# Selective scan beside a mixture of experts: decaying states kept in PSUM, every read-out on VectorE, one product for ranks and rows

## What is computed

```python
# L3 attention (E = 256 channels, N = 16 states, rank 64, after an RMS norm and a causal convolution)
xs    = silu(conv(x @ in_w.T) + conv_b)
delta = softplus(xs @ wd1.T @ wd2.T + wd2_b)
A     = -exp(A_log)                      # 256 x 16
Bm, Cm = xs @ wb.T, xs @ wc.T            # 16 numbers per token each
# per token l, channel e, state n:
h[e,n] = exp(delta[e] * A[e,n]) * h[e,n] + (delta[e] * xs[e]) * Bm[n]
y[e]   = sum over n of h[e,n] * Cm[n]
out    = resid + ((y + xs * W_D) * silu(skip)) @ out_w.T
# L3 ffn: 8 experts, 128 -> 512 -> 128, relu, top-p gates; every expert runs on every token
y = sum over e of gate[e] * (relu(x @ W1[e] + b1[e]) @ W2[e] + b2[e])
```

## Time and profile before

| | us |
|---|---|
| median of 3 runs | 2452.4 |
| lowest, highest | 2448.72, 2458.42 |
| the profiled execution, its own time | 2451.05 |
| its span, first to last instruction | 2449.3 |
| TensorE busy (share of the span) | 2167.2 (88%) |
| VectorE busy | 1669.1 (68%) |
| ScalarE busy | 1234.2 (50%) |
| GpSimd busy | 1018.8 (42%) |
| first scan starts, last scan starts | 1560.2, 2327.2 |

### The profile page before, as it was taken

One profiled execution on the slowest core, in us unless ns is written; L12 is line 12 of the kernel. 1 busy time (PEld: TensorE's weight loads), 2 busy tenths in 40 slices (PEclk: granted clock), 3 DMA queues, 4 the chain that ended last, 5 costly groups with the idle time before them and its releaser, 6 DMA issues. The chain is left out here.

```text
span 2449.3 us, 33072 instructions
## 1 busy us (share of the span) xinstructions
PE 2167.2 (88%) x11302; PEld 1547.8 (63%) x11302; DVE 1669.1 (68%) x3253; ACT 1234.2 (50%) x2710; POOL 1018.8 (42%) x815
## 2 busy tenths in 40 slices
PE   7888777899799999999997595767999999999998
PEld 3565556688698988898897484322554545545554
DVE  6667555677666676667765694599687877869921
ACT  6231222499544454554453352556566565655543
POOL 5000000121122233233322463689687777868722
PEclk9799899899899999999998696898999999999999
DMA  9500000000000000000000234333333324334311
GB/s 352 165 1 0 1 1 1 1 1 1 20 1 1 1 11 11 1 11 11 9 4 11 68 104 161 97 112 97 108 104 96 113 91 117 110 94 121 95 35 35
DMA packets 77151, 145.25 MB, mean 59 GB/s; under 512 B 9432, under 2 KB 31080, under 8 KB 75944
## 3 DMA queue, kind: packets, MB, share of 16 engines
q1 hardware_dynamic: 72600, 133.67, 17.7%
q0 software_dynamic: 4384, 9.46, 1.2%
HBM read 130.91 MB, written 31.65 MB: 66 GB/s over the span
## 5 line engine op out<-in xcount | busy, mean ns | idle before, releaser
L224 ACT ACTIVATE TMP<-ps,W 128x512 f32<-128x512 f32 (+2 forms) x784 | 457.1, 614 | 391.5 <-PE ps L209 225.6
L209 PE MATMUL ps<-TMP,W 128*128 128x512 f32 (+5 forms) x1232 | 612.8, 604 | 42.3 <-ACT TMP L227 9.4
L209 PE MATMUL ps<-TMP 128*128 128x65 f32 (+5 forms) x4354 | 514.9, 286 | 6.6 <-DVE W L229 4.4
L209 PEld LDWEIGHTS ps<-TMP 128*128 128x128 f32 (+3 forms) x4354 | 474.6, 192 | 52.5 <-issue 17.5
L233 POOL TENSOR_TENSOR TMP<-TMP 128x512 f32<-128x512 f32 (+1 forms) x176 | 227.9, 1298 | 588.0 <-ACT TMP L224 435.6
L209 PEld LDWEIGHTS ps<-TMP,W 128*128 128x128 f32 (+3 forms) x1232 | 218.3, 188 | 250.7 <-issue 152.8
L233 POOL TENSOR_TENSOR TMP<-TMP,W 128x512 f32<-128x512 f32 x256 | 356.9, 1418 | 30.4 <-DVE TMP L2874 29.3
L209 PE MATMUL ps<-TMPr,Wr 128*128 128x512 f32 x768 | 320.0, 524 | 5.6 <-ACT TMP L224 5.6
L209 PE MATMUL ps<-TMPr 128*128 128x512 f32 (+4 forms) x1032 | 266.3, 404 | 34.0 <-DVE TMPr L229 23.1
L209 PEld LDWEIGHTS ps<-TMPr 128*128 128x128 f32 (+2 forms) x1032 | 192.9, 197 | 84.3 <-issue 23.2
L209 PEld LDWEIGHTS ps<-TMPr,Wr 128*128 128x128 f32 x768 | 145.0, 190 | 140.9 <-issue 116.0
(11 more groups left out here) (239 smaller groups left out, 3114.3 us busy)
## 6 DMA issues: line engine op xcount, KB each, us to landing
W<-rows SPq DMA_DIRECT2D x224, 256.0 KB, 3.6
sorted<-pad SPq DMA_DIRECT2D x8, 2304.0 KB
XK<-gates SPq DMA_DIRECT2D x64, 256.0 KB, 3.5
TMP<-rows SPq DMA_DIRECT2D x32, 256.0 KB, 3.3
TMP<-sorted SPq DMA_DIRECT2D x72, 72.0 KB, 2.0
W<-wp SPq DMA_DIRECT2D x1, 4124.0 KB, 14.8
XK<-results SPq DMA_DIRECT2D x16, 256.0 KB, 3.8
W<-wp SPq DMA_DIRECT2D x1, 3072.0 KB, 27.1
```

The costliest lines, as they stand in the source:

```text
L209: return nc.tensor.matmul(out, lhsT, rhs, start=start, stop=stop, **k)
L224: return nc.scalar.activation(out, x, f, bias=bias, scale=scale)
```

## The change

- The scan writes its result over its own decay operand, `Ab[x]` in PSUM; the four buffers `Hb` are gone.
- Every read runs on VectorE, right behind its scan in the list, with `Ab[x]` (PSUM) as its second operand; `by_pool` and GpSimd's reads are gone. There are 8 buffers `Cb` instead of 6.
- `carry` reads the last column from `Ab[x]` and waits for the read; `decay` of the next state waits for the read of the state before, and for the carry's copy, where there is one.
- `rank` and `bc` become one product with 96 output rows (`wnT`), copied by one `rank_out` into one of two tiles `Nw`. `delta` multiplies all 96 rows, with zeros in the 32 rows of `wd2T` that face B and C; `rows_out` stores rows 64 to 95.
- `first_unit` is 59 instead of 58, and most steps beside are one slot later.
- `tail` of a slot comes 4 slots after its scan (as before), `output` one slot later than before.

```diff
-     ... ("wd1T", 128, 128), ("wd2T", 64, 256), ("wd2b", 128, 2), ("wbcT", 128, 64), ...
+     ... ("wnT", 128, 192), ("wd2T", 96, 256), ("wd2b", 128, 2), ...
-        Bb, Cr, Ub, Hb, Cb = (more(n) for n in (4, 4, 6, 4, 6))
-        narrow = ar(512)
-        d1, Bw = narrow[0:64, :], [narrow[64 + 32 * j:96 + 32 * j, :] for j in range(2)]
+        Bb, Cr, Ub, Cb = (more(n) for n in (4, 4, 6, 8))
+        Nw = [ar(512) for _ in range(2)]
-        by_pool = lambda g: g % 16 % 3 == 1
-        first_unit = 32 + 26
+        first_unit = 32 + 27
-            put(q + 8, ("rank", i))
-            put(q + 9, ("rank_out", i), ("bc", i))
-            put(q + 10, ("bc_out", i))
+            put(q + 9, ("rank", i))
+            put(q + 10, ("rank_out", i))
...
             if 0 <= g < GN:
-                plan.append(("scan", (g, s)))
-                if s:
-                    plan.append(("read", (g, 0)))
+                plan += [("scan", (g, s)), ("read", (g, s))]
             plan += gated(u - 2) + joined(u - 3)
-            if 0 <= g - 2 < GN:
-                plan.append(("tail", (g - 2, s)))
-                if (g - 2) % 16 == 15:
-                    plan.append(("output", ((g - 2) // 16, s)))
+            if 0 <= q - 4 < 2 * GN:
+                plan.append(("tail", divmod(q - 4, 2)))
+            if 0 <= q - 5 < 2 * GN and (q - 5) // 2 % 16 == 15:
+                plan.append(("output", ((q - 5) // 32, (q - 5) % 2)))
             plan += beside.pop(q, [])
             if 0 <= g + 1 < GN:
                 plan.append(("decay", (g + 1, s)))
-            if s and 0 <= g < GN:
-                plan.append(("read", (g, 1)))
             plan += down(u - 1)
...
                     for x in range(2):
-                        r = mm(bank(step, a)[0:64, :], w("wd1T")[:, x * 64:(x + 1) * 64], ch(sets[a % 2][1], x), x == 0, x == 1)
+                        r = mm(bank(step, a)[0:96, :], w("wnT")[:, 96 * x:96 * x + 96], ch(sets[a % 2][1], x), x == 0, x == 1)
...
-                    mm(bank(step, a), tile(w("wd2T"), x), d1).then_inc(*de_pe(a))
+                    mm(bank(step, a), tile(w("wd2T"), x), Nw[i % 2][0:96, :]).then_inc(*de_pe(a))
...
-                e.wait_ge(*h_dve.at((g, x)))
-                acopy(car[:, j:j + 1], Hb[(2 * g + x) % 4][:, 511:512]).then_inc(*c_act((g, x)))
+                e.wait_ge(*hc_dve.at((g, x)))
+                acopy(car[:, j:j + 1], Ab[x][:, 511:512]).then_inc(*c_act((g, x)))
...
                     if g:
-                        e.wait_ge(*h_dve.at((g - 1, x)))
+                        e.wait_ge(*hc_dve.at((g - 1, x)))
+                        if (g - 1) // 16 % 2 == 0:
+                            e.wait_ge(*c_act.at((g - 1, x)))
                     act(Ab[x], ch(sets[i % 2][2], x), ACT.Exp, scale=negA[:, x * 16 + n:x * 16 + n + 1]).then_inc(*a_act(a))
...
-                    nc.vector.tensor_tensor_scan(Hb[q % 4], Ab[x], Ub[q % 6], first, ALU.mult, ALU.add).then_inc(*h_dve(a))
-                elif step == "read" and not by_pool(a[0]):
+                    nc.vector.tensor_tensor_scan(Ab[x], Ab[x], Ub[q % 6], first, ALU.mult, ALU.add).then_inc(*h_dve(a))
+                elif step == "read":
                     g, x = a
                     q = 2 * g + x
                     e.wait_ge(*h_dve.at(a))
...
-                    tt(Cb[q % 6], Cr[g % 4], Hb[q % 4], ALU.mult).then_inc(*hc_dve(a))
+                    tt(Cb[q % 8], Cr[g % 4], Ab[x], ALU.mult).then_inc(*hc_dve(a))
...
-                    gtt(Cb[q % 6], Cr[g % 4], Hb[q % 4], ALU.mult).then_inc(*hc_pool(a))
```

More of the change, by code:

```diff
@@ L2365, in hand_over @@
             n = norm(7, i)
[L2366 to L2384, removed]
+            put(q + 6, ("out", i))
+            put(q + 7, ("result", i))
+            put(q + 8, n[0])
+            put(q + 9, n[1])
+            put(q + 10, n[2])
+            put(q + 11, n[3])
+            put(q + 13, n[4])
+            put(q + 14, n[5])
+            put(q + 15, n[6])
+            put(q + 16, n[7], ("split", i))
+            put(q + 17, ("shift", i))
+            put(q + 19, ("probs", i))
+            put(q + 20, ("route", (i, 0)))
+            put(q + 21, ("route", (i, 1)))
+            put(q + 23, ("route", (i, 2)))
+            put(q + 25, ("row", i))
+            put(q + 26, ("row_out", i))
+            put(q + 28, ("table", i))
+            put(q + 29, *[("fetch", 8 * i + k) for k in range(3)])
         def norm_ahead(i, q):
@@ L2407, in scan_moe_stage @@
         plan += both("shut") + norm(6, 1)[:3]
-        plan += [("rank", 0), ("bc", 0), ("rank_out", 0), ("bc_out", 0)] + both("delta")
+        plan += [("rank", 0), ("rank_out", 0)] + both("delta")
         plan += [("softplus", (0, 0)), ("softplus", (0, 1)), ("exp", 0), ("log", 0), ("dx", 0), ("rows_out", 0)]
@@ L2483, in scan_moe_stage @@
         I = range(NCH)
-        rk_pe, rk_act, bc_pe, ex_act, ln_act, dl_dve, dx_pool, out_pe, res_dve = (
-            Sig(sem("s7_" + n), I) for n in ("rank_pe", "rank", "bc_pe", "delta_exp", "delta_log", "delta", "dx", "out_pe", "out"))
+        rk_pe, rk_act, ex_act, ln_act, dl_dve, dx_pool, out_pe, res_dve = (
+            Sig(sem("s7_" + n), I) for n in ("rank_pe", "rank", "delta_exp", "delta_log", "delta", "dx", "out_pe", "out"))
         de_pe, mx_act, ab_act = (Sig(sem("s7_delta_" + n), of(plan, "delta")) for n in ("pe", "max", "abs"))
@@ L2489, in scan_moe_stage @@
         GE = [(g, e) for g in G for e in range(2)]
[L2490 to L2493, removed]
+        a_act, u_pool, h_dve, hc_dve, y_pe = (Sig(sem("s7_" + n), GE) for n in ("decay", "input", "state", "read", "y_sum"))
         c_act = Sig(sem("s7_carried"), [(g, e) for g, e in GE if g // 16 % 2 == 0])
@@ L2520, in scan_moe_stage @@
         for s, a in plan:
-            if s in ("open", "conv", "rank", "bc", "delta", "centre", "back", "back2", "logits", "out", "row"):
+            if s in ("open", "conv", "rank", "delta", "centre", "back", "back2", "logits", "out", "row"):
                 takers.append((s, a))
-        first_bank = {("conv", (0, 0)): 7, ("conv", (0, 1)): 5, ("rank", 0): 6, ("bc", 0): 4, ("delta", (0, 0)): 7, ("delta", (0, 1)): 5,
+        first_bank = {("conv", (0, 0)): 7, ("conv", (0, 1)): 5, ("rank", 0): 6, ("delta", (0, 0)): 7, ("delta", (0, 1)): 5,
                       }
@@ L2532, in scan_moe_stage @@
             holder[bank_no(*t)] = t
-        let_go = {"open": gt_dve, "conv": ev_act, "rank": rk_act, "bc": raw_act, "delta": ab_act, "back": n_xa, "back2": n_xk,
+        let_go = {"open": gt_dve, "conv": ev_act, "rank": rk_act, "delta": ab_act, "back": n_xa, "back2": n_xk,
                   "logits": n_lgs, "out": res_dve, "row": rw_act}
```

81 lines of the change are left out of this document (29 added, 52 removed), and 2 rows, old and new, of the table GROUPS.

## The result

The changed kernel takes 2464.3 us (median of 7 runs, 2461.2 to 2465.8), the kernel before, beside it on the same chip, 2452.4: a ratio of 1.0042, with an interval of 1.0029 to 1.0055. The forecast was 2431, in a range of 2412 to 2460, and the measured time lies above that range. It became slower, by a little less than the 0.5% that I had taken for measurable, though the interval lies wholly above 1. The profiled execution took 2462.4 us around a span of 2460.6, against 2451.1 and 2449.3.

A forecast was written before the change was run, and what follows sets the result against it. VectorE and GpSimd were taken to bound the lead, VectorE the routing stretches, TensorE the rest. The terms -4.7 - 6.0 - 8.6 - 1.0 + 1.1 - 1 (last 32 scan slots) gave -20.2, so 2431 us, range 2412 to 2460.

The forecast's parts named there:

- One slot later: Whole last stage: a lead slot more (2.4), a common slot less (3.3), an end slot more (2.0); +1.1 us.
- Routing stretches: VectorE-bound stretch of each 32-slot block in the common part: reads -0.7, contention -1.0, chain +0.7; six stretches, -6.0 us.
- three hand-overs between engines: In the chain from scan over read and ScalarE to the next decay: about 0.08 us each, an estimate.
- The lead: First 56 scans, bound by VectorE and GpSimd: reads -4.7, decay waits +2, less contention -2; -4.7 us in all.
- a bound of 12: Sign of being wrong: VectorE waiting more than 12 us for decays in the lead, against 6.9 before.
- One product: One matmul product less per chunk, 1.7 us: -8.6 where TensorE bounds, -1.0 ahead of the first scan.
- The scan in PSUM: Every scan: writing its output to PSUM costs 0 more, taken from ScalarE's rows.
- That rival: Scan pays for its output in PSUM: 1.74 us per scan, 2494 us in all, slower; chance 0.12.
- The dependent pair: Each read right behind its scan: gap 0.03, no overlap; 0.12 us per slot, 6.7 in the lead.
- the rival without it: A dependent read costs no more than any other: lead 6.7 less, six routing stretches 1.0 each, 2418; chance 0.06.
- The rival by ScalarE's chain: Each of 24 long ScalarE stays costs the lost slack, 1.1 us; 2451, no change; chance 0.15.

The follow-up runs named there:

- e1: The changed kernel with all steps beside back in their old slots (first_unit 58); 2445.1 us, ratio 0.9977 to the kernel before.
- e4: The kernel before with `rank` and `bc` as one product with 96 rows and nothing else; 2435.6 us, ratio 0.9934 to the kernel before.
- e8b: e1 with each slot's read moved behind the steps beside, as the slot's last VectorE work; ratio 0.9932 to the kernel before.
- e7: The changed kernel with only `open`, its copy and its gate one slot later; 2446.3 us, ratio 0.9952 to the kernel before.
- e5b: e5a with each read right behind its scan, states still in SBUF; ratio 1.0075 to the kernel before.
- e5c: e5b with decay and carry waiting for the read in place of the scan, states in SBUF; ratio 1.008 to the kernel before.
- e5a: e4 with all reads on VectorE at their old places in the list, states in SBUF; 2449.9 us, ratio 0.9976 to the kernel before.
- e13: The changed kernel with only each slot's decay moved ahead of its steps beside in the lists; ratio 0.9982 to the kernel before.

## Why the prediction was wrong

**One slot later, +1.1: the step that failed, by 18 us.** I priced the slots by their mean lengths. e1 measures the move at 19.6 us in the changed kernel (16 by the ratios). What a slot holds was to be read, not how long it is: the change moves `log` one slot and leaves `square` and `open`, so ScalarE's 3.7 us between the table loads now end in what TensorE needs next. The rule that I had written down myself, what stands behind a long stay in an engine's list and who waits for it, I applied to the decay and not to the moved steps.

**Routing stretches, -6.0: wrong in sign.** From e4 to e1, which is states in PSUM with every read on VectorE behind its scan (and more buffers), the common part grows from 609.8 to 623.7. The stretch with the routing, in e4 and in e1:

```profile
1977.60:2006.50 28.90, 25.87 (x77) 13.20 (x76) 27.16 (x46) 20.70 (x51) 25.87 (x21) 1.00 0.25 83
```

```profile
1976.40:2005.90 29.50, 24.25 (x71) 12.19 (x70) 25.95 (x49) 20.92 (x50) 19.86 (x18) 1.00 0.24 82
```

VectorE has 1.2 us less to do, where the forecast had 1.7 (0.7 and 1.0), but waits 2.9 us for one decay behind the logarithm instead of 1.3, a loss of 1.6 where 0.7 was counted. The stretch gains nothing, and over the block TensorE idles for 5.2 instead of 3.0. Over the whole common part it idles 9.0 us longer (28.9 against 19.9) and is busy 4.9 longer, at a mean clock of 0.99 instead of 1.00: the 13.9 us. By e8b, 5.9 of them are the reads' place in the list; of the remaining 8.0, 4.2 are idle time and 3.8 busy time, and what is behind them is open. The three hand-overs between engines, put at 0.08 each, take 0.03 each in the traces, so the chain itself was not priced too low by them.

**The lead, -4.7: about right in e1 (-4.0 against the kernel before, -5.3 against e4), not in the changed kernel**, where it is -1.6. VectorE's waits for decays are 13.5 us there and 9.1 in e1, and I had put a bound of 12 on them. They aren't the whole cause: e7 has 13.3 us of them and a lead of 136.9.

**One product, -8.6 and -1.0: right in kind, too small.** e4's last stage is 14.6 shorter than before; the term missing was the change of size, 1.4 us per chunk. The first scan comes 0.5 us (e4), 0.9 (the changed kernel) and 1.5 (e1) earlier, for the -1.0.

**The scan in PSUM, 0:** 17 ns each, 4 us over 256 scans. That rival falls. **The dependent pair, 0.03 and no overlap:** as measured after, 1.25 from scan to read; the rival without it falls, as far as the single instructions show. The Trainium skill, page "VectorE: DVE Perf Modes", section "The DRAIN you can't avoid", has eight copies that take 13.88 us with a semaphore after each or only after the last. Here the pair with a wait has a gap of 0.03 and the pair without one overlaps by 0.09, so this trace does not agree with it for these instructions.

**The rival by ScalarE's chain** was nearest: long stays of ScalarE do eat the saving. But I let them cost slack only, with its place at the read-to-decay chain, which by itself costs 3.6 us with states in SBUF (e5b to e5c), and ended it at no change. Put together for the last stage: -14.6 (product) + 7.2 (reads and PSUM, e4 to e1) + 19.6 (slots) = +12.2, the measured 901.3 less 889.1.

## What to carry to other kernels

A step moved by one slot is not priced by the slot's length. List what stands behind every long stay of the engine that it is moved on (here a function between two table loads), and look whether a product of the fullest engine comes next to it. A gap of the fullest engine can cost twice, once as a stall and, in some blocks here, once in clock. And a shorter list for one engine can be lost in its waits for another, as VectorE's here in waits for ScalarE. Of the four parts of this change the plainest, two narrow products made into one, was by itself (0.9934) worth as much as the best run with states in PSUM and every read on VectorE (e8b, 0.9932).

## What was not expected of the hardware

- A change of matmul size between 128 and 64 or 32 (columns of weights, or rows) takes 0.09 us more at each edge in the starts of fp32 records (0.52 against 0.43, in the kernel before); between 128 and 96 none (0.43 in e4).
- In SBUF a read's length depends on where it stands: 1096 ns in e5a and 869 in e5b in the mean of 192, where one in PSUM always takes 687. No run separates here which instructions of GpSimd it meets.
- A wait of 3.4 us of TensorE for the same copy is followed by the low clock in one of four cases in the changed kernel (0.53, and three times 1.00), and in two of four in e13. What decides it, no run here shows.
- The table loads beside the logarithm are 2.6 us of each chunk. The Trainium skill, page "ScalarE: Activation LUTs", section "Table sets: the hidden batching unit", names a set that holds both exponential and logarithm; no run here tries it.
